# A graph layer's node stage taken apart: its table rows made during the index search, its q and k products beside the edge tiles

## The chip, the cores and the metric

One core of a Trainium2 chip runs the whole program. Its engines work in parallel, each through its own queue of instructions, and meet at semaphores: TensorE (PE in the rows; PEld is its weight load), VectorE (DVE), ScalarE (ACT), GpSimd (POOL) and SyncE (SP, which here only starts DMA transfers). The metric is the device time of one execution in microseconds.

## The reference

One layer over 6250 nodes of 256 channels and 106250 directed edges, sorted by destination. With xn the row-normalised x, it computes x + GNN(xn) + MIX(xn), and then adds a routed expert network of the result.

```python
h = (x @ W.T).reshape(n, H, D)                      # GNN, x is xn
alpha = einsum(h_src, a_src) + einsum(h_dst, a_dst)
enc = relu(edge_attr @ edge_W.T + edge_b)
alpha = alpha + sum(enc * h_dst, axis=-1)           # then leaky relu, softmax over each node's edges
out = segment_sum(h_src * attn[..., None], dst)     # + bias
q, k, v = split(x @ W_qkv + b_qkv)                  # MIX, x is xn
q = q - mean(q); k = k - mean(k); q2 = q*q; k2 = k*k
k2 = l2_normalize(k2 / (sum_c k2 + 1e-7), over nodes)
q2 = l2_normalize(q2 / (sum_c q2 + 1e-7), over channels)
out = (v + q2 @ (k2.T @ v) / sqrt(N)) @ W_out + b_out
```

The experts: a second normalisation, the two best of 8 per node, gelu between two products.

## The kernel before, in words

Nodes are worked on in 49 tiles of 128 (NT; the last has 106). The program is a series of blocks; between two blocks all engines meet at a barrier.

**The search** (lines 233 to 520). For each node the place of its first edge in the sorted list is found in two steps: a coarse count against every 277th destination (L377, DVE), then the row of 277 destinations is gathered for each node (L300, POOL, 49 indirect DMAs) and counted (L437). PE gives each node its successor's value (L326, L327), so that its degree is known (L444). Nodes are then ranked by degree with large one-hot tables on DVE (L449 to L470) and PE (L329 to L336), so that a tile holds nodes of like degree. At the same time DVE and ACT split the edge attributes into three bf16 parts (`records`, L396 to L410, and L346) and SP writes them to DRAM (`recs`). DVE also centres the weights (L386 to L394) and PE makes two small weight products (L314 to L321): `wmo` folds W_v and W_out into one.

**The node stage** (L523 to L732). x is loaded, and for each tile, in an overlapped loop over tiles with buffers for two: DVE normalises (L670 to L676), PE turns the rows (L585) and makes three products (L594): q and k (`wqk`, 512 columns), the table row (`whs`, 272 columns: h and its two attention parts), and v through W_out (`wmo`). ACT and DVE square and scale q and k (L639 to L647, L684 to L708). PE adds the tile into k2.T @ xn and two column sums that stay in PSUM (L603 to L607). SP stores the table rows (L565) and q2 (L567). After the last tile the sums become `kvo` (L621, L721 to L732), which the router needs.

**The edge stage** (L743 to L1003), in the order of ranked tiles. POOL fetches for tile t+1 the edge records (L801) and the destinations' table rows (L803), and gathers one table row per edge slot for 128 nodes at a time (L807, up to 36 slots). Slots go in groups of four; a tile has between 2 and 9 groups (GMAX), 230 in all 49 tiles, and steps of a group above the second stand in an `If` on a number that each engine loads from `info`. PE turns the records (L845), ACT copies them out of PSUM (L902, L904), PE encodes a group's attributes (L854, `encode`), DVE makes the scores (L932, L935, `score`), ACT the exponentials (L917), DVE the weighted rows (L943, `weigh`), and PE sums them (L863, `collect`). Scores of tile t+1 and weights of tile t alternate on DVE. The rows of a tile go to one of two halves of `hbuf`: POOL waits at a tile's start until DVE has weighed the tile before last (`msg_ready`). DVE clears `hbuf` first (L993).

**The router** adds the aggregated rows and q2 @ kvo (L1335) to x; the experts follow.

The order on each engine is the order in which the code is written. The steps touched are those of the search and edge blocks on all five engines.

## Time and profile before

| | us |
|---|---|
| median of 3 runs (lowest, highest) | 3477.73 (3471.06, 3493.76) |
| the profiled execution | 3464.38 |
| its span | 3462.6, granted clock 0.775 in the mean |
| DVE busy | 1726.2 |
| PE busy | 2056.6 |
| POOL busy | 1251.7 |
| ACT busy | 500.4 |

A row of a timeline that ends in brackets tells how long the engine had been idle and what ended it: an engine's instruction, a transfer (DMA), `issue` (nothing that the profile shows) or `remote` (an event without a known sender).

### The profile page before, as it was taken

The numbers are of one execution on the slowest core, as the hardware profiler recorded it, in microseconds if no ns is written. First come the engines' busy times: TensorE is split into PE (matmuls) and PEld (weight loads), VectorE is DVE, ScalarE is ACT, GpSimd is POOL, SyncE is SP. The second block draws the span as 40 slices with busy tenths as digits, with TensorE's granted clock in tenths as the row PEclk, the third lists the DMA queues.
The fourth block names the chain that finished last, engine by engine and source line by source line (L and its number), as shares of the span: only waits on it lengthen the run. The fifth ranks groups of instructions, "written<-read, shape, count | busy, mean of one in ns | idle before, by whom it ended". The sixth has DMA issues, their size and how long they took to land. (4 is left out here: it accounts for less than half of the span.)

```text
span 3462.6 us, 35916 instructions
## 1 busy us (share of the span) xinstructions
PE 2056.6 (59%) x8311; PEld 1568.4 (45%) x8312; DVE 1726.2 (50%) x3708; ACT 500.4 (14%) x1336; POOL 1251.7 (36%) x1251
## 2 busy tenths in 40 slices
PE   0038887355555455444444444445555999999996
PEld 0026555233333333333333322224444888888885
DVE  5756666667655566555555555465453112221221
ACT  0103333000000000000000000002222222222221
POOL 5000000555555555544555544433543221222211
PEclk9569999566666667766666677677566999999998
DMA  4121111333333333322333322224332222322223
GB/s 129 79 80 39 37 37 39 91 87 95 92 88 83 88 93 88 88 78 76 85 87 84 89 74 74 79 59 164 115 112 89 59 60 60 62 37 57 58 39 98
DMA packets 145579, 270.85 MB, mean 78 GB/s; under 512 B 27546, under 2 KB 104068, under 8 KB 144708
## 3 DMA queue, kind: packets, MB, share of 16 engines
q0 software_dynamic: 71312, 179.36, 20.7%
q1 hardware_dynamic: 66292, 77.89, 7.0%
q10 hardware_dynamic: 7872, 12.58, 1.1%
q14 instruction: 82, 0.67, 0.1%
q8 instruction: 21, 0.34, 0.0%
HBM read 208.02 MB, written 68.11 MB: 80 GB/s over the span
## 5 line engine op out<-in xcount | busy, mean ns | idle before, releaser
L807 POOL DMA_INDIRECT hbuf<-table,recb x847 | 805.8, 951 | 736.7 <-issue 689.1
L863 PE MATMUL psum<-msg,ident 128*128 128x256 f32 x1840 | 639.9, 515 | 690.2 <-DVE msg L943 533.0
L863 PEld LDWEIGHTS psum<-msg,ident 128*128 128x128 f32 x1840 | 475.5, 267 | 879.6 <-DVE msg L943 602.3
L932 DVE SCALAR_TENSOR_TENSOR prod<-psum,hd 128x1024 f32<-128x1024 f32 x230 | 281.1, 1222 | 276.8 <-remote 210.5
L943 DVE TENSOR_TENSOR msg<-hbuf,psum 128x1024 f32<-128x1024 f32 x230 | 274.8, 1212 | 248.0 <-remote 235.4
L1378 PE MATMUL psum<-f_xT,fw 128*128 128x256 f32 x1664 | 380.3, 387 | 26.9 <-issue 14.7
L1315 POOL DMA_INDIRECT acc<-yo,id_now x104 | 161.4, 1552 | 633.9 <-DVE yo L1587 606.7
L1388 PE MATMUL psum<-fw,hT 128*128 128x256 f32 x1664 | 367.8, 379 | 0.0
L1378 PEld LDWEIGHTS psum<-f_xT,fw 128*128 128x128 f32 x1664 | 322.3, 194 | 77.8 <-issue 19.1
L1388 PEld LDWEIGHTS psum<-fw,hT 128*128 128x128 f32 x1664 | 312.1, 190 | 40.3
L935 DVE TENSOR_REDUCE al<-prod 128x32 f32<-128x1024 f32 x230 | 280.6, 1220 | 7.9
L1429 ACT ACTIVATE hT<-psum,fb 128x256 f32<-128x256 f32 x416 | 195.0, 473 | 592.2 <-PE psum L1378 531.7
L902 ACT COPY recT<-psum 128x512 bf16<-128x512 bf16 x49 | 28.7, 585 | 1479.0 <-PE psum L845 873.2
L854 PE MATMUL psum<-ew,recT 128*128 128x512 bf16 x460 | 180.1, 506 | 60.2 <-ACT recT L904 21.6
L801 POOL DMA_INDIRECT recb<-recs,stg x49 | 46.6, 951 | 448.8 <-ACT stg L898 399.7
L1574 DVE COPY id_now<-id_next 128x2 int32<-128x2 int32 x52 | 8.8, 169 | 361.7 <-POOLq L1318 359.5
L1584 DVE TENSOR_TENSOR yo<-psum,fb 128x256 f32<-128x256 f32 x104 | 44.1, 424 | 212.7 <-PE psum L1388 212.7
L1303 POOL DMA_INDIRECT xs<-xstage,pstage x98 | 95.9, 978 | 132.5 <-DVEq L1495 104.8
L845 PE MATMUL psum<-ident_bf,recb 128*128 128x128 bf16 x441 | 42.2, 256 | 167.0 <-issue 150.6
L594 PE MATMUL psum<-wqk,xT 128*128 128x512 f32 x196 | 102.2, 646 | 29.6 <-ACT xT L633 29.6
L845 PEld LDWEIGHTS psum<-ident_bf,recb 128*128 128x128 bf16 x441 | 32.0, 115 | 189.8 <-issue 171.8
L854 PEld LDWEIGHTS psum<-ew,recT 128*128 128x128 bf16 x460 | 49.9, 118 | 123.6 <-issue 41.6
(304 smaller groups left out, 2295.8 us busy)
## 6 DMA issues: line engine op xcount, KB each, us to landing
xr<-xs SPq DMA_DIRECT2D x53, 260.0 KB, 2.7
hbuf<-table,recb POOLq DMA_INDIRECT x847
fw<-in_w ACTq DMA_DIRECT2D x12, 1024.0 KB
table<-tab SPq DMA_DIRECT2D x49, 136.0 KB
recs<-rec SPq DMA_DIRECT2D x3, 2216.0 KB, 6.7
q2d<-q2r SPq DMA_DIRECT2D x49, 128.0 KB, 1.7
aggs<-oo SPq DMA_DIRECT2D x49, 128.0 KB
qrow<-q2d SPq DMA_DIRECT2D x49, 128.0 KB
```

The source lines that it names most:

```text
L594: mm = pe.matmul(ps[:, 0:width], xT[:, b, P * o:P * o + P], w[:, o, :], start=(o == 0), stop=(o == 1))
L807: pool.indirect_dma_start(hbuf[:, b, s, :], None, table, bass.IndirectOffsetOnAxis(ap=rec_i[:, b, s, REC // 2 - 1:REC // 2], axis=0)).then ...
L854: mm = pe.matmul(psum[:, 1024 * (k % 2) + 512 * q:1024 * (k % 2) + 512 * q + 512], recT[:, b, k, :], ew[:].rearrange("p s c -> p (s c)")[: ...
L863: mm = pe.matmul(AC[:, 0:C], ident[:], msg[:, k % 2, s, :], start=(k == 0 and s == 0), stop=False, skip_group_check=True)
L932: v.scalar_tensor_tensor(out=prod[:, k % 2, :, :], in0=Z[k % 2], scalar=0.0, in1=bc(hd[:, b, 0:C], 1, GS), op0=ALU.max, op1=ALU.mult).then ...
L935: v.tensor_reduce(al[:, b, GS * HEADS * k:GS * HEADS * (k + 1)], prod[:, k % 2, :, :].rearrange("p s (h d) -> p (s h) d", h=HEADS), AX.X, ...
L943: v.tensor_tensor(msg[:, k % 2, :, :].rearrange("p s (h d) -> p s h d", h=HEADS), hbuf[:, b, s, 0:C].rearrange("p s (h d) -> p s h d", h=H ...
L1303: pool.indirect_dma_start(xs, bass.IndirectOffsetOnAxis(ap=pstage[:, i % 2, k, j:j + 1], axis=0), xstage[:, s, :], None).then_inc(st_x[s], 16)
L1315: pool.indirect_dma_start(acc, bass.IndirectOffsetOnAxis(ap=id_now[:, r:r + 1], axis=0), yo[:, r, :], None, compute_op=ALU.add).then_inc(s ...
L1378: mm = pe.matmul(HB[m % 4][:, 0:FT], fw1[:, e % 2, o, P * m:P * m + P], xT[:, o, :], start=(o == 0), stop=(o == 1))
L1388: mm = pe.matmul(bank[5 + r][:, 0:C], hT[:, m, P * r:P * r + P], fw2[:, e % 2, m, :], start=(m == 0), stop=(m == FM - 1))
L1429: act.activation(hT[:, m, :], HB[m % 4][:, 0:FT], ACT.Gelu, bias=fb1[:, FM * e + m:FM * e + m + 1]).then_inc(gelu_done, 1)
```

## The change

The node stage is gone. Its parts go to two places. In the search block x is loaded early, DVE takes the statistics of seven tiles at a time between the pieces of the coarse search, ACT normalises and makes the copies out of PSUM, and PE runs a loop of 49 tiles, written out, that makes the table row and v; bias and x are added to v by matmuls in PSUM, so that ACT's copy puts the finished row into `xm`. The normalised rows are also stored (`xnd`). ACT takes over the casts of the edge attributes and starts their stores. In the edge block SP loads a tile of normalised rows per edge tile, PE turns it, makes q and k behind the third `encode`, and adds the sums of the tile before at the end of the tile; ACT squares and scales; q2 is stored without its row factor, which the router applies (`qscale`). The records are turned in one PSUM bank (8 blocks, then the ninth) to make room for the accumulators. Only the parts of `hbuf` that must be zero are cleared. The closing steps stand behind the last edge tile.

```diff
-                        for k in range(3):
-                            sp.wait_ge(rec_copied, k + 1)
...
-                            sp.dma_start(recs_v[:, RG * k:RG * k + RG, :], rec[:]).then_inc(st_rec, 16)
-                        sp.wait_ge(st_rec, 48)
...
+                        for c in range(2, NT // NC):
+                            load_x(c)
+
+                        for t in range(NT):
+                            sp.wait_ge(xn_ready, t + 1)
+                            sp.dma_start(xnd[t * P:t * P + P, :], xn[:, t % 4, :]).then_inc(st_xn[t % 4], 16)
+                            sp.wait_ge(tab_ready, t + 1)
+                            sp.dma_start(table[t * P:t * P + P, :], tab[:, t % 2, :]).then_inc(st_tab[t % 2], 16)
...
-                        pe.wait_ge(prep_ready, 1)
+                        pe.wait_ge(ld_w, 16 * 8)
+                        pe.wait_ge(rep_ready, 1)
...
                         mm.then_inc(prep_mm, 1)
+                        pe.wait_ge(prep_ready, 1)
+
+                        for t in range(NT + 1):
+                            if t < NT:
+                                pe.wait_ge(xn_ready, t + 1)
+                                after(pe, xt_ready, t - 1)
+                                for o in range(2):
+                                    mm = pe.transpose(XT[t % 2][:, P * o:P * o + P], xn[:, t % 4, P * o:P * o + P], ident[:])
+                                mm.then_inc(xt_mm, 1)
+                            s = t - 1
+                            if s >= 0:
+                                pe.wait_ge(xt_ready, s + 1)
+                                after(pe, tab_ready, s - 1)
+                                for o in range(2):
+                                    mm = pe.matmul(HP[s % 2], xT[:, s % 2, P * o:P * o + P], whs[:, o, :], start=(o == 0), stop=(o == 1))
+                                mm.then_inc(h_mm, 1)
+                                after(pe, m_added, s - 1)
+                                pe.matmul(MP[s % 2], ones[0:1, :], bmo[0:1, :], start=True, stop=False, skip_group_check=True)
+                                pe.matmul(MP[s % 2], ident[:], xm[:, s, :], start=False, stop=False, skip_group_check=True)
+                                for o in range(2):
+                                    mm = pe.matmul(MP[s % 2], xT[:, s % 2, P * o:P * o + P], wmo[:, o, :], start=False,
+                                                   stop=(o == 1), skip_group_check=True)
+                                mm.then_inc(m_mm, 1)
...
+                        pe.wait_ge(m_added, NT)
...
+                                act.activation(xn[:, t % 4, :], xm[:, t, :], ACT.Identity, bias=off[:, t:t + 1],
+                                               scale=rs[:, t:t + 1]).then_inc(xn_ready, 1)
+                            s = t - 1
+                            if 0 <= s < NT:
+                                act.wait_ge(xt_mm, s + 1)
+                                after(act, m_mm, s - 1)
+                                act.copy(xT[:, s % 2, :], XT[s % 2]).then_inc(xt_ready, 1)
+                            s = t - 2
+                            if 0 <= s < NT:
+                                act.wait_ge(h_mm, s + 1)
+                                after(act, st_tab[s % 2], 16 * (s // 2))
+                                act.copy(tab[:, s % 2, :], HP[s % 2]).then_inc(tab_ready, 1)
+                                act.wait_ge(m_mm, s + 1)
+                                act.copy(xm[:, s, :], MP[s % 2]).then_inc(m_added, 1)
...
+                        for c in range(NT // NC):
+                            ts = slice(NC * c, NC * c + NC)
+                            act.wait_ge(var_ready, c + 1)
+                            act.activation(sd[:, ts], mv[:, ts, 1], ACT.Sqrt, bias=eps[:, 0:1]).then_inc(sd_ready, 1)
+                            pieces[c]()
+                            for t in range(3 * c, 3 * c + 3):
+                                step(t)
...
+                                ch.step(v.bn_stats(st[:, t - NC * c, :], xm[:, t, :]))
+                            for t in range(NC * c, NC * c + NC):
+                                ch.lag(NC - 1)
+                                ch.step(v.bn_aggr(mv[:, t, :], st[:, t - NC * c, :]))
+                            ch.wait()
+                            v.sem_inc(var_ready, 1)
...
+                        ch.run(v.tensor_tensor(bmo[:], bout[:], gbias[:], ALU.add))
+                        v.sem_inc(rep_ready, 1)
+                        blocks(1)
+                        stats(0)
+                        norm(0)
+                        v.wait_ge(prep_copied, 1)
+                        ch.run(v.tensor_tensor(bmo[:], bmo[:], bvo[:], ALU.add))
+                        v.sem_inc(prep_ready, 1)
+                        pieces = {1: (0, 0), 2: (0, 1), 4: (1, 0), 5: (1, 1)}
+                        for c in range(1, NT // NC):
+                            stats(c)
+                            if c + 1 < NT // NC:
+                                blocks(c + 1)
+                            norm(c)
+                            if c in pieces:
+                                rest(*pieces[c])
...
-            with ExitStack() as nd:
...
+                            after(sp, q_ready, t + 1)
+                            sp.dma_start(q2d[bass.ds(t * P, P), :], qsq[:]).then_inc(st_q, 16)
+                            if not is_last(t):
+                                after(sp, g_mm, t)
+                                load(t + 1, 1 - b)
...
+
+                        def project(t):
+                            after(pe, xte_ready, t + 1)
+                            pe.matmul(QK[:], ones[0:1, :], bqk[0:1, :, :].rearrange("p a c -> p (a c)"), start=True, stop=False,
+                                      skip_group_check=True)
+                            for o in range(2):
+                                mm = pe.matmul(QK[:], xTe[:, P * o:P * o + P], wqk[:, o, :, :].rearrange("p a c -> p (a c)"),
+                                               start=False, stop=(o == 1), skip_group_check=True)
+                            mm.then_inc(qk_mm, 1)
...
+                        def sums(t, b, n):
+                            after(pe, k4_ready, t + 1)
+                            for o in range(2):
+                                pe.matmul(GP[:, C * o:C * o + C], xrow[0:n, b, P * o:P * o + P], kn[0:n, :],
+                                          start=False, stop=False, skip_group_check=True)
+                                pe.matmul(CP[:, o:o + 1], kn[0:n, P * o:P * o + P], ones[0:n, 0:1],
+                                          start=False, stop=False, skip_group_check=True)
+                                mm = pe.matmul(CP[:, 2 + o:3 + o], k4[0:n, P * o:P * o + P], ones[0:n, 0:1],
+                                               start=False, stop=False, skip_group_check=True)
+                            mm.then_inc(g_mm, 1)
...
                             n, before = groups_of(pe, t), 0 if is_at(t, 0) else groups_before(pe, t)
+                            after(pe, sq_done, t)
...
                                 turn(t + 1, 1 - b)
-                                after(pe, rec_ready, 2 * t + 4)
+                                after(pe, rec_ready, 2 * t + 3)
                                 for k in range(2):
                                     encode(1 - b, k, upto)
+                                turn_last(t + 1, 1 - b)
+                            transposed(t, b)
...
+                                if k == 2:
+                                    project(t)
                                 with pe.If(n > k):
                                     collect(b, k, before)
-
+                            if not is_at(t, 0):
+                                sums(t - 1, 1 - b, P)
...
+                        sums(NT - 1, (NT - 1) % 2, LAST)
...
+                        def squares(t):
+                            after(act, qk_mm, t + 1)
+                            act.activation(ksq[:], QK[:, C:2 * C], ACT.Square, accum_out=ksum[:]).then_inc(ksq_ready, 1)
+                            after(act, st_q, t * 16)
+                            act.activation(qsq[:], QK[:, 0:C], ACT.Square,
+                                           accum_out=qsum[:, bass.ds(t, 1), 0]).then_inc(q_ready, 1)
+                            after(act, q_ready, t + 1)
+                            act.activation(QK[:, C:2 * C], qsq[:], ACT.Square,
+                                           accum_out=qsum[:, bass.ds(t, 1), 1]).then_inc(sq_done, 1)
...
+                            after(act, g_mm, t - 1)
                             act.activation(pr[:, 0:CAP * HEADS], al[:, b, 0:CAP * HEADS], ACT.Exp).then_inc(exp_ready, 1)
+                            after(act, xt_mm, t + 1)
+                            act.copy(xTe[:], QK[:, 0:C]).then_inc(xte_ready, 1)
+                            if not is_at(t, 0):
+                                scaled(t - 1)
+                            squares(t)
...
                             if not is_at(t, 0):
+                                factor(t - 1)
...
-                        v.memset(hbuf[:], 0.0).then_inc(hbuf_clear, 1)
+                        v.memset(prod[:, 0, :, :], 0.0).then_inc(zero_ready, 1)
+                        v.memset(hbuf[:, :, 0:GS - 1, :], 0.0).then_inc(hbuf_clear, 1)
+                        v.memset(hbuf[:, :, GS - 1:CAP, C:C + HEADS], 0.0).then_inc(hbuf_clear, 1)
...
-                            v.tensor_tensor(row, row, MX[f % 2][:, 0:C], ALU.add).then_inc(x2_ready, 1)
+                            v.scalar_tensor_tensor(out=row, in0=MX[f % 2][:, 0:C], scalar=qscale[:, f:f + 1], in1=row,
+                                                   op0=ALU.mult, op1=ALU.add).then_inc(x2_ready, 1)
```

On PE, in the search block before: the small weight products (L321) are followed by the successor matmuls (L326, L327).

```order
L314 MATMUL psum<-wout,wvT 128x256 x4
L317 MATMUL psum<-wout,bvrep 128x256 x2
L321 MATMUL psum<-asd,wh 128x16 x4
L326 MATMUL psum<-first,shift 128x49
L327 MATMUL psum<-first,wrap 128x49
L329 MATMUL psum<-small,tri 128x64
```

PE at the end of the same block's table loop, now (L371 is the table product, L374 bias, L375 x, L377 v):

```order
L377 MATMUL psum<-wmo,xT 128x256 x2
L371 MATMUL psum<-whs,xT 128x272 x2
L374 MATMUL psum<-bmo,ones 128x256
L375 MATMUL psum<-xm,ident 128x256
L377 MATMUL psum<-wmo,xT 128x256 x2
L382 MATMUL psum<-first,shift 128x49
L383 MATMUL psum<-first,wrap 128x49
```

The successor matmuls (L382, L383) now stand behind the loop of 49 tiles.

PE in one tile of the edge loop before, down to the third group:

```order
L845 MATMUL psum<-ident_bf,recb 128x128 x9
L77 REGISTER_ALU
L854 MATMUL psum<-ew,recT 128x512 x4
L77 REGISTER_ALU
L863 MATMUL psum<-msg,ident 128x256 x4
L77 REGISTER_ALU
L863 MATMUL psum<-msg,ident 128x256 x4
L880 COMPARE_AND_BRANCH
L77 REGISTER_ALU
L854 MATMUL psum<-ew,recT 128x512 x2
L880 UNCONDITIONAL_BRANCH
L882 COMPARE_AND_BRANCH
```

The same tile now (L833 turns x, L838 and L841 are bias and the q and k product):

```order
L833 MATMUL psum<-ident,xrow 128x128 x2
L78 REGISTER_ALU
L826 MATMUL psum<-msg,ident 128x256 x4
L78 REGISTER_ALU
L826 MATMUL psum<-msg,ident 128x256 x4
L872 COMPARE_AND_BRANCH
L78 REGISTER_ALU
L817 MATMUL psum<-ew,recT 128x512 x2
L872 UNCONDITIONAL_BRANCH
L838 MATMUL psum<-bqk,ones 128x512
L841 MATMUL psum<-wqk,xTe 128x512 x2
L876 COMPARE_AND_BRANCH
```

The new product has moved in between the third group's encode (L817) and its collect.

## Rows read from the trace of the kernel before

**Rows 1.** Stages: stretch, its us, busy us and instructions per engine, clock, DMA share, GB/s

```profile
0.00:142.90 142.90, 8.57 (x26) 6.22 (x27) 86.82 (x277) 17.58 (x8) 47.10 (x54) 0.78 0.36 126
142.90:214.40 71.50, 15.53 (x102) 15.15 (x102) 60.75 (x69) 0.00 (x0) 0.49 (x1) 0.60 0.00 0
214.40:239.40 25.00, 2.29 (x4) 1.17 (x4) 0.78 (x3) 1.28 (x1) 0.00 (x0) 0.50 0.81 256
239.40:598.60 359.20, 298.11 (x1282) 212.60 (x1282) 234.65 (x890) 122.20 (x491) 0.00 (x0) 0.96 0.11 37
598.60:621.80 23.20, 3.46 (x15) 1.44 (x15) 18.61 (x4) 1.51 (x4) 1.91 (x2) 0.50 0.07 19
621.80:2350.30 1728.50, 829.13 (x2728) 555.87 (x2726) 1018.80 (x1179) 83.40 (x194) 896.89 (x943) 0.69 0.31 84
```

**Rows 2.** Timeline, search stage: start, us, engine, line, operation, output<-input, idle before

```profile
50.21 0.17 DVE L380 TENSOR_SCALAR blk<-blk 128x7 f32<-128x7 f32 x1 [7.64 <-issue]
...
71.28 3.78 PE L314 MATMUL psum<-wout,wvT 128*128 128x256 f32 x8 [62.85 <-issue]
...
73.89 1.26 POOL L300 DMA_INDIRECT rows_b<-in_dst,blki  x1 [0.30 <-issue]
...
142.93 0.21 DVE L444 TENSOR_TENSOR deg<-psum,first 128x49 f32<-128x49 f32 x1 [1.24 <-PE psum L327]
...
216.69 5.49 SPq L557 DMA_DIRECT2D xm<-in_x  x3
```

**Rows 3.** Timeline, PE in one tile of the node stage

```profile
405.67 1.96 PE L594 MATMUL psum<-wqk,xT 128*128 128x512 f32 x4 [0.61 <-ACT xT L633]
...
407.46 1.08 PE L594 MATMUL psum<-whs,xT 128*128 128x272 f32 x4
...
408.38 1.03 PE L594 MATMUL psum<-wmo,xT 128*128 128x256 f32 x4
...
409.25 0.59 PE L603 MATMUL psum<-k2n,xn 128*128 128x256 f32 x2
...
410.69 0.36 PE L607 MATMUL psum<-ones,k 128*128 128x1 f32 x2
```

**Rows 4.** Groups of the node stage: count, busy us, mean ns, idle before and its releaser

```profile
L585 PE MATMUL psum<-ident,xn 128*128 128x128 f32 x98 | 21.6, 303 | 47.1 <-DVE xn L676 47.1
...
L633 ACT COPY xT<-psum 128x256 f32<-128x256 f32 x49 | 18.2, 372 | 126.7 <-PE psum L585 126.7
```

**Rows 5.** Timeline, PE in the node stage's first tile

```profile
242.31 3.78 PE L594 MATMUL psum<-wqk,xT 128*128 128x512 f32 x4 [0.46 <-ACT xT L633]
```

**Rows 6.** Timeline, end of the node stage and start of the edge stage, DVE

```profile
591.33 0.16 DVE L721 COPY cols<-psum 128x4 f32<-128x4 f32 x1 [1.05 <-PE psum L607]
...
602.75 16.38 DVE L993 MEMSET hbuf<- 128x19584 f32 x1 [4.62 <-issue]
...
620.09 1.22 DVE L932 SCALAR_TENSOR_TENSOR prod<-psum,hd 128x1024 f32<-128x1024 f32 x1 [0.34 <-issue]
```

**Rows 7.** Groups of the edge stage, DVE's waits

```profile
L932 DVE SCALAR_TENSOR_TENSOR prod<-psum,hd 128x1024 f32<-128x1024 f32 x229 | 279.9, 1222 | 276.5 <-remote 210.5 <-PE psum L854 41.5 <-issue 19.1
...
L943 DVE TENSOR_TENSOR msg<-hbuf,psum 128x1024 f32<-128x1024 f32 x230 | 274.8, 1212 | 248.0 <-remote 235.4 <-PE psum L863 12.5
```

**Rows 8.** Timeline of the edge stage at four places

```profile
716.56 1.22 DVE L943 TENSOR_TENSOR msg<-hbuf,psum 128x1024 f32<-128x1024 f32 x1 [2.81 <-PE psum L863]
...
1200.72 0.95 POOL L807 DMA_INDIRECT hbuf<-table,recb  x1 [0.30 <-issue]
...
1204.76 1.22 DVE L943 TENSOR_TENSOR msg<-hbuf,psum 128x1024 f32<-128x1024 f32 x1 [7.36 <-remote]
...
1210.96 0.94 POOL L807 DMA_INDIRECT hbuf<-table,recb  x1 [9.30 <-issue]
...
2300.34 1.23 DVE L932 SCALAR_TENSOR_TENSOR prod<-psum,hd 128x1024 f32<-128x1024 f32 x1 [25.36 <-remote]
```

**Rows 9.** The page's list of transfers

```profile
q2d<-q2r SPq DMA_DIRECT2D x49, 128.0 KB, 1.7
```

507 lines of the change are left out of this document (236 added, 271 removed).

## The prediction

> **What bounds the kernel now.** I read the stages first, then each stage's own limit. The split by stages [rows 1] has six rows: the search for node boundaries up to 142.9 us, its ranking part up to 214.4, a load of x, the node stage (359.2 us), the clearing of hbuf, and the edge stage (1728.5 us); routing and the experts follow and hardly change. The reader should see two things. In the ranking part PE and ACT work for 15.5 and 0.0 of 71.5 us, and in the first part for 8.6 and 17.6 of 142.9. The node stage is the reverse: PE is busy 298 of 359 us at a granted clock of 0.96, and POOL and the DMA engines do next to nothing. In the edge stage no engine is full: DVE 1019 of 1728 us, PE 829, POOL 897, ACT 83.
>
> The timeline of one node tile [rows 3] shows what a tile costs on PE when its parts follow one another: the q and k product starts at 405.67, the table product at 407.46, the v product at 408.38, the sums at 409.25, and the last of the sums ends at 410.69 + 0.36 = 411.05. So q and k take 1.79 us, the table 0.92, v 0.87 and the sums 1.80. With the two turns (21.6 / 49 = 0.44, [rows 4]) that is 5.8 of the 359.2 / 49 = 7.3 us of a tile.
>
> The edge stage's limit is a loop through three engines [rows 8]. POOL issues its last gather of a burst at 1200.72 and then waits for DVE's products; DVE has stood still for 7.36 us and goes on at 1204.76, 3.1 us after that gather was issued; POOL starts the next burst at 1210.96. At 2300.34 DVE has waited 25.36 us for the end of a burst. These waits, whose releaser the profile doesn't know (it writes remote), sum to 210.5 + 235.4 = 446 us ahead of DVE's two large instructions [rows 7], 9 us for each of 49 tiles. The early tiles are without them; there DVE waits for PE (2.81 us at 716.56, [rows 8]).
>
> **The change, part by part.**
>
> *Removed: the node stage.* The next stage starts at 598.6 instead of some 3 us behind the search (a barrier: the search ends at 214.3 here and x is asked for at 216.69, [rows 2]). What remains of the node work must fit in the search stage and in the edge stage.
>
> *Added to the search: the table loop on PE.* PE does per tile two turns (0.44), the table product (0.92), and the sum of bias, x and v. The last is twice the matmuls of the v product alone (0.87), so 1.74. Sum: 3.10 us if nothing waits; by the node stage's busy times, which include each drain, 3.6. I take 3.3, so 49 x 3.3 = 162 us. ACT carries four copies of 256 to 272 columns per tile at 0.37 [rows 4], about 1.6 us with their gaps, under PE's 3.3, plus some 25 us of record casts. DVE adds 49 pairs of statistics, about 30 us, to a part in which it had 56 of 142.9 us free: hidden. The loop starts when weights, the first seven tiles of x and their statistics are there: PE's small products take about 6 us before, DVE's first statistics about 5 after two blocks of boundary search. I put it at 38 us. It ends at 200; with 5 us for the casts that stand in ACT's queue between the copies, at 205.
>
> *What waits for it.* The matmul that gives each node its successor stands behind the whole loop in PE's queue (the first piece of order above). Before, DVE had its answer at 142.93 [rows 2]; now at 205 + 1.3 = 206. DVE itself would be ready near 130. Behind it stand the ranking steps, unchanged: 71.5 us to the end of the block. So the edge stage starts at 206 + 71.5 + 3 = 280.5 instead of 598.6: **-318 us**.
>
> *Clearing.* The fill of all of hbuf takes 16.38 us [rows 6] and DVE's first score waits for it (620.09). The new fills are 2 x 3 x 272 and 2 x 33 x 8 columns, 2160 of 19584, so 1.8 us, and prod's 0.9: **-14 us**.
>
> *Added to the edge tile.* On PE: two turns of x (0.44), a bias matmul (0.45), q and k (1.79), sums (1.80): 4.5 us at the high clock. At the low clock q and k took 3.78 us against a busy time of 1.95 in the steady tile [rows 5], a factor of 1.94, so 8.7 us. The product goes behind the third encode; there PE stands still while DVE waits for the burst, 7 us in the tile shown, so it is covered. The sums come at the tile's end, before the next tile's records are turned: 1.8 to 3.5 us, of which about 1 us is slack ahead of DVE's score. DVE gets two one-column steps, 0.4 us with their gap. So DVE reaches its long wait about 2.5 us later, and since that wait ends with the burst, the tile isn't longer. Where no such wait stands (the first half dozen tiles, and the last) I count 4 us each, 28, and 2 for odd ones: **+30 us**. If the cover were gone, all 4.9 us would be on the path in 49 tiles: 240. SP gets a store and a load of 128 KB per tile; the load waits for the sums of the tile before and is wanted after the next tile's second encode, some 5 us later, against 1.7 us for such a transfer to land [rows 9]. POOL's queue gets nothing.
>
> *Moved to the end.* The closing steps (from 591.33 to 598.1, [rows 6]) now stand behind the last edge tile, and ACT loads a table for them: 6.8 and a little over 1 for that, **+8 us**. The router's scaling rides in an instruction that was there: 0.
>
> The sum: 3464.4 - 318 - 14 + 30 + 8 = 3170 us in the profiled execution's measure. That execution was 13.3 us under the median of the three runs shown, 3477.7, so I predict **3184 us**.
>
> **Operations that this trace doesn't show.** A matmul with one row of weights (the biases): between nothing and a full one of the same columns; I take the full one, which its streamed columns suggest (0.45 and 0.22 us each; low end -32 us over both loops). ACT's record copies are the same 1152 columns in two pieces, cut elsewhere: taken as equal; they lie ahead of the covered wait either way. A start of the table loop before 25 us isn't possible (weights and statistics), after 75 neither (next paragraph).
>
> **A rule against the edge part.** In the search stage DVE stood still for 7.64 us before L380 in straight code, waiting for nothing but its own instruction, while POOL issued row gathers; PE began its products at 71.28, near the last gather at 73.89 [rows 2]. The same may befall the new unrolled loops. The Trainium skill (Runtime: NRT & Kernel Launch, Instruction fetch mechanics) says that straight code is fetched ahead and its fetch mostly hidden, and that a taken branch whose target isn't resident stalls for a DMA. By that rule the unrolled table loop would be free of such stalls and the sum stays as it is, while the edge loop, now longer on PE and ACT, could get new ones; the row at L380 speaks against the first half.
>
> **Rivals.**
> - *The table loop is held by the row gathers.* PE gets going only as the gathers end, at 75 instead of 38, as its first product did in this trace. +37: 3221. It speaks for it that PE waited until 71.28; against it, that PE then waited for DVE. 13%.
> - *The table loop runs at the low clock or in a handshake with ACT.* 3.3 x 1.94 = 6.4 us per tile, +152: 3336. The node stage held 0.96 with PE busy 83%, and the loop is denser. 6%.
> - *The edge additions aren't covered, at the high clock.* 49 x 4.9 = 240 in place of 30: 3394. 6%.
> - *Slower than before.* The added matmuls run at the low clock (the edge stage's granted clock is 0.69) and the wait of DVE isn't tied to the burst but to PE or to DVE's own code, so that everything added lies on the path: 8.7 + 0.4 + 1.5 for exp, which is now behind the ninth record block on ACT. 49 x 10.6 = 520 in place of 30: 3674. It decides from 6.6 us of exposed work per tile on: (3477.7 - 3184 + 30) / 49. 4%.
> - *Full exposure between these two*, within 1% of before: 3%.
> - *A warmer PE shortens the edge stage.* DVE's waits for PE there (41.5 + 12.5 = 54 us, [rows 7]) go as PE is less idle: 3184 - 30 - 54 = 3100. 8%.
>
> That the change doesn't do what it says isn't likely: the order of instructions shows the node loop gone. The forecast keeps 60%.
>
> **Range and chances.** The forecast's own range is 3130 to 3245: -32 for cheap biases, -20 for an earlier start, +37 and some tiles more for the other side. To hold 8 in 10 the range takes in the warmer edge stage's half and reaches toward the slow table loop: 3105 to 3310. Differences under 1% can't be told from no change here. Faster by more than 1%: all cases but two, 0.93; within 1%: 0.03; slower: 0.04.
>
> **What will show it.** The first successor matmul's answer near 206 us; PE busy over 90% from 40 to 205 us at a clock above 0.9; first staging copy of the edge stage near 280; first score 6 to 9 us behind it; an edge stage of 1755 us or so from the first gather on, with DVE's unexplained waits shorter by about 2.5 us each. I'm wrong if PE has gaps in the table loop, if DVE's waits in the edge stage keep their length while its other work grows, or if PE's new project step shows before DVE's fourth score.

## The result: 0.943 of the kernel before

The changed kernel takes 3277.96 us (median of 4 runs, 3275.74 to 3294.0) against 3476.05 us before on the same chip: ratio 0.9431, 95% interval 0.9407 to 0.9455. The forecast was 3184 us with a range of 3105 to 3310, so the gain was 198 us and not 292. The time lies outside the forecast's own range of 3130 to 3245 and inside the wide one. The profiled execution spans 3274.2 us against 3462.6; these two are compared below.

The split by stages of the changed kernel answers to [rows 1]. Columns: stretch, its length, busy time of PE, its weight loads, DVE, ACT and POOL, granted clock, DMA share, GB/s.

```profile
0.00:26.00 26.00, 7.75 (x22) 5.54 (x23) 16.75 (x72) 5.46 (x10) 9.94 (x14) 0.96 0.86 280
26.00:154.00 128.00, 94.49 (x325) 62.26 (x325) 75.28 (x305) 62.88 (x113) 39.21 (x40) 0.79 0.49 166
154.00:241.90 87.90, 87.90 (x366) 61.46 (x366) 0.00 (x0) 38.71 (x104) 0.00 (x0) 0.96 0.29 105
241.90:317.70 75.80, 15.38 (x104) 14.88 (x103) 60.76 (x69) 0.24 (x2) 0.48 (x1) 0.62 0.00 0
326.10:2158.10 1832.00, 1036.51 (x3718) 691.64 (x3716) 1035.82 (x1294) 211.86 (x639) 893.92 (x942) 0.72 0.32 86
2158.10:3274.20 1116.10, 896.72 (x4156) 773.44 (x4156) 308.47 (x1287) 274.56 (x639) 305.16 (x251) 0.88 0.32 78
```

The table loop has two halves. From 154 us on PE is busy without a gap; in the 128 us before it is busy 94.5 at a clock of 0.79. Then DVE ranks with little work on the other engines, as before. Against the kernel before:

| stretch | before | after | difference |
|---|---|---|---|
| up to the first staging copy of the edge stage | 598.6 | 317.7 | -280.9 |
| from there to DVE's first score | 21.5 | 8.45 | -13.0 |
| first score to the last tile's output | 1726.3 | 1816.3 | +90.0 |
| from there to the router's first gather | 4.6 | 15.6 | +11.0 |
| router and experts | 1111.6 | 1116.1 | +4.5 |

**The search stage.** Eight rows of the changed kernel's timeline (start, length, engine, line, operation; in brackets how long the engine had been idle and what ended it):

```profile
145.65 1.89 ACT L431 CAST rec<-att 128x831 bf16<-128x831 f32 x1 [3.96 <-DVE att L494]
147.57 5.28 ACT L436 COPY rec<-rec 128x2493 bf16<-128x2493 bf16 x2
...
151.78 0.21 DVE L582 SCALAR_TENSOR_TENSOR first<-blk,fine 128x49 f32<-128x49 f32 x1
...
153.98 0.69 PE L364 MATMUL psum<-ident,xn 128*128 128x128 f32 x2 [9.44 <-ACT xn L407]
...
238.72 0.37 ACT L420 COPY xm<-psum 128x256 f32<-128x256 f32 x1 [1.73 <-PE psum L377]
241.76 0.37 ACT L420 COPY xm<-psum 128x256 f32<-128x256 f32 x1 [1.73 <-PE psum L377]
242.14 0.21 DVE L586 TENSOR_TENSOR deg<-psum,first 128x49 f32<-128x49 f32 x1 [90.15 <-PE psum L383]
...
317.68 0.29 ACT L907 COPY stg<-fetch 128x2 int32<-128x2 int32 x2 [75.56 <-PEq L169]
```

ACT casts the last piece of a third of the records, copies it twice (5.28 us) and issues its store. PE has no normalised tile in this time and stands 9.44 us. From 160.53 on ACT's copies of the finished row (`xm`) come 3.25 us apart, 26 of them, and the loop ends at 242. DVE had its first positions at 151.78 and waited 90.15 us for the successor product, which stands behind the loop on PE. The answer at 242.14 and the 75.5 us of ranking behind it give the start.

**The edge stage.** The costliest groups that answer to [rows 7], and ACT's and POOL's (busy and mean ns of one; idle time before them by releaser). The name `DMA srci<-in_src` is that of a semaphore number used earlier in the program: the profile knows no sender, as where it writes `remote`.

```profile
L769 POOL DMA_INDIRECT hbuf<-table,recb x847 | 805.1, 951 | 527.3 <-issue 511.8 <-DVE msg L985 15.5
L974 DVE SCALAR_TENSOR_TENSOR prod<-psum,hd 128x1024 f32<-128x1024 f32 x230 | 281.4, 1223 | 563.4 <-DMA srci<-in_src 373.2 <-PE psum L817 150.3 <-issue 33.9
L985 DVE TENSOR_TENSOR msg<-hbuf,psum 128x1024 f32<-128x1024 f32 x230 | 278.4, 1211 | 39.4 <-remote 24.1 <-PE psum L826 9.2 <-ACT psum L942 5.6
L911 ACT COPY recT<-psum 128x1024 bf16<-128x1024 bf16 x49 | 49.6, 1012 | 784.1 <-DMA bndi<-in_dst 632.3 <-PE psum L806 105.0 <-issue 46.8
L763 POOL DMA_INDIRECT recb<-recs,stg x49 | 46.3, 944 | 348.5 <-issue 246.5 <-DVEq L1004 82.0 <-ACT stg L907 20.0
```

DVE's idle time ahead of its two large instructions rose from 524.5 us to 602.8, which is 78 of the 90 us. Its unexplained part fell (446 to 397), but the waits for PE's encode rose from 41.5 to 150.3. The tile at 837.9 us shows why:

```profile
837.86 0.62 PE L806 MATMUL psum<-ident_bf,recb 128*128 128x128 bf16 x8 [1.10 <-issue]
837.88 0.46 DVE L1002 TENSOR_TENSOR al<-al,mask 128x288 f32<-128x288 f32 x1 [2.20 <-issue]
...
841.97 0.94 POOL L769 DMA_INDIRECT hbuf<-table,recb  x1 [0.30 <-issue]
...
844.56 1.01 ACT L911 COPY recT<-psum 128x1024 bf16<-128x1024 bf16 x1 [12.03 <-DMA bndi<-in_dst]
845.62 1.89 PE L817 MATMUL psum<-ew,recT 128*128 128x512 bf16 x4 [7.15 <-ACT recT L911]
846.69 1.23 DVE L974 SCALAR_TENSOR_TENSOR prod<-psum,hd 128x1024 f32<-128x1024 f32 x1 [4.13 <-PE psum L817]
...
847.82 0.20 ACT L907 COPY stg<-fetch 128x2 int32 x1
...
849.79 0.94 POOL L763 DMA_INDIRECT recb<-recs,stg  x1 [6.88 <-issue]
...
852.28 0.95 POOL L769 DMA_INDIRECT hbuf<-table,recb  x1 [0.30 <-issue]
...
860.55 0.59 PE L817 MATMUL psum<-ew,recT 128*128 128x512 bf16 x2
...
871.05 0.94 POOL L769 DMA_INDIRECT hbuf<-table,recb  x1 [0.30 <-issue]
...
875.21 1.22 DVE L974 SCALAR_TENSOR_TENSOR prod<-psum,hd 128x1024 f32<-128x1024 f32 x1 [15.54 <-DMA srci<-in_src]
```

PE turns the records at the tile's start, but ACT's first record copy comes 6.7 us later, 1.6 us behind the end of POOL's burst. The staging copy stands behind the second record copy, which needs PE's ninth transpose, which stands behind four encode matmuls: 3.3 us behind the first copy (before the change 1.1, in the tile at 939.2 us of its trace, below). So POOL fetches the next records 11.9 us into the tile, its late burst starts so late that the next tile's first eight gathers follow without a gap (16 gathers, 852.28 to 871.99), and DVE's last score waits to their end plus 3.2 us. PE's encode for that score (L817, the row at 860.55) had been done at 861.1 us. The next tile is short: in this pair 42.4 and 25.5 us stand where two of 31.5 stood.

```profile
941.08 0.58 ACT L902 COPY recT<-psum 128x512 bf16<-128x512 bf16 x1 [25.63 <-PE psum L845]
941.62 0.69 ACT L904 COPY recT<-psum 128x640 bf16<-128x640 bf16 x1
942.20 0.20 ACT L898 COPY stg<-fetch 128x2 int32 x1
```

The pairs aren't all of the 90 us. Tile by tile against the kernel before, 9 us lie in the first 5 tiles, 44 in the next 16, where the long and short tiles alternate, 28 in the 10 behind them, and 5 in the 17 after those.

### The profile page after: what moved, and what is told of

The parts are those of the page before. It is cut to its first block and busy times, and to the rows that moved or that the text cites. A ratio compares the mean times of both kernels' runs of the same rounds, so it can differ in the third digit from the quotient of the medians.

```text
span 3274.2 us, 35308 instructions
## 1 busy us (share of the span) xinstructions
PE 2143.4 (65%) x8703; PEld 1611.7 (49%) x8704; DVE 1500.5 (46%) x3029; ACT 595.3 (18%) x1505; POOL 1252.5 (38%) x1251
## 3 DMA queue, kind: packets, MB, share of 16 engines
q0 software_dynamic: 71312, 179.36, 22.0%
## 5 line engine op out<-in xcount | busy, mean ns | idle before, releaser
L826 PE MATMUL psum<-msg,ident 128*128 128x256 f32 x1840 | 590.5, 484 | 454.0 <-DVE msg L985 453.0
L826 PEld LDWEIGHTS psum<-msg,ident 128*128 128x128 f32 x1840 | 450.9, 250 | 600.6 <-DVE msg L985 489.1
L817 PE MATMUL psum<-ew,recT 128*128 128x512 bf16 x460 | 172.1, 487 | 190.5 <-ACT recT L911 179.8
L985 DVE TENSOR_TENSOR msg<-hbuf,psum 128x1024 f32<-128x1024 f32 x230 | 278.4, 1211 | 39.4 <-remote 24.1
L911 ACT COPY recT<-psum 128x1024 bf16<-128x1024 bf16 x49 | 49.6, 1012 | 784.1 <-DMA bndi<-in_dst 632.3
L817 PEld LDWEIGHTS psum<-ew,recT 128*128 128x128 bf16 x460 | 47.4, 113 | 247.7 <-ACT recT L911 188.6
L923 ACT ACTIVATE ksq<-psum 128x256 f32<-128x256 f32 x49 | 18.8, 383 | 606.4 <-remote 289.9
L841 PE MATMUL psum<-wqk,xTe 128*128 128x512 f32 x196 | 97.2, 618 | 0.0
```

The lines of the kernel that those rows point to most:

```text
L817: mm = pe.matmul(psum[:, 1024 * (k % 2) + 512 * q:1024 * (k % 2) + 512 * q + 512], recT[:, b, k, :], ew[:].rearrange("p s c -> p (s c)")[: ...
L826: mm = pe.matmul(AC[:, 0:C], ident[:], msg[:, k % 2, s, :], start=(k == 0 and s == 0), stop=False, skip_group_check=True)
L841: mm = pe.matmul(QK[:], xTe[:, P * o:P * o + P], wqk[:, o, :, :].rearrange("p a c -> p (a c)"), start=False, stop=(o == 1), skip_group_che ...
L985: v.tensor_tensor(msg[:, k % 2, :, :].rearrange("p s (h d) -> p s h d", h=HEADS), hbuf[:, b, s, 0:C].rearrange("p s (h d) -> p s h d", h=H ...
```

## The experiments

"Stage" is the time from the first staging copy to the router's first gather: 1752.4 us before (14 of it the clearing of hbuf), 1840.4 in the changed kernel. The runs fell on other chips than the prediction's. The kernel before took 3530.6, 3523.7 and 3527.8 us on the three chips of runs 1 to 4, 5 to 8 and 9 to 11, so these three are compared with each other, though the expectations of the third speak of one chip. "Ratio" is to the kernel before on the run's own chip, with its 95% interval.

| run | start of stage | stage | ratio |
|---|---|---|---|
| 5 the changed kernel again | 323.5 | 1861.6 | 0.9392 (0.936 to 0.9425) |
| 1 no node work | 319.7 | 1699.6 | 0.9007 (0.8973 to 0.9041) |
| 2 staging copy first | 318.5 | 1786.7 | 0.9171 (0.9135 to 0.9207) |
| 3 ranking inside the loop | 265.0 | 1865.6 | 0.9222 (0.9192 to 0.9253) |
| 4 before, with ACT filler | 608.8 | 1805.7 | 1.0035 (1.0019 to 1.0051) |
| 6 plain loads | 321.1 | 1424.9 | 0.8155 (0.813 to 0.8181) |
| 7 no node work, two banks | 321.5 | 1779.2 | 0.9231 (0.9203 to 0.926) |
| 8 three edits | 276.3 | 1783.6 | 0.9039 (0.9007 to 0.9071) |
| 9 pause on POOL | 322.5 | 1848.8 | 0.938 (0.935 to 0.9409) |
| 10 three edits, spread | 241.1 | 1784.6 | 0.8965 (0.8932 to 0.8997) |
| 11 no node work, staging first | 318.5 | 1766.0 | 0.9215 (0.9183 to 0.9246) |
| 12 twelve gathers first | 234.4 | 1385.0 | 0.9074 (0.9054 to 0.9094) |

In runs 1, 6, 7 and 11 the router gets other rows, and in runs 1, 7 and 11 the part from its first gather on is 18 to 25 us longer than in run 5; of these four only the stage is read.

**Run 1, no node work.** `transposed`, `project`, `sums`, `scaled`, `squares` and `factor` are gone from the tiles, with SP's load of the normalised rows, and q2d's store writes a constant.

```diff
-                            after(pe, sq_done, t)
...
-                            transposed(t, b)
...
-                                if k == 2:
-                                    project(t)
...
-                                sums(t - 1, 1 - b, P)
```

> The changed kernel without the node work in its edge tiles: the xn row's load and transposes, the q and k products, the three squares, the scaled copies, the factor and the sums are left out (so the global branch gets no sums, and the router sees other rows); what stays is the record turn through one bank, the last transpose behind two encodes, and DVE's new order. Read from the first staging copy to the router's first gather, which is 1840.4 us in the changed kernel and 1752.4 in the one before (1738 without the clearing of hbuf). Theory A, the node work itself delays the tiles: 1730 to 1760. Theory B, the one-bank turn with its last copy behind two encodes delays them: it stays at 1815 to 1840. A mixture lies between, and its place gives the shares.

Measured 1699.6, below theory A's range; theory B, that the one-bank turn alone costs the time, is out. But ACT's first record copy is still late in many tiles (8.3 us into the one at 862.4), and in the tile of the same number as the one at 837.9 POOL's bursts run together as there: 18 issues without a gap, from 814.36 to 836.57. Four rows:

```profile
814.36 0.94 POOL L759 DMA_INDIRECT recb<-recs,stg  x1 [6.84 <-issue]
...
829.11 1.23 DVE L956 SCALAR_TENSOR_TENSOR prod<-psum,hd 128x1024 f32<-128x1024 f32 x1 [4.92 <-DMA srci<-in_src]
829.37 0.95 POOL L765 DMA_INDIRECT hbuf<-table,recb  x1 [0.30 <-issue]
...
835.62 0.95 POOL L765 DMA_INDIRECT hbuf<-table,recb  x1 [0.30 <-issue]
```

DVE's wait ends here after 4.92 us, in the middle of the gathers, and the pair takes 34.7 and 25.4 us. So bursts that run together don't by themselves make the tiles long.

**Run 2, staging copy first.** `turned_last` is the second half of `turned`, the wait for PE's ninth transpose and the copy behind it.

```diff
                                 after(act, ld_hd[b], 8 * (t - b) + 16)
                                 stage(t + 2, b)
+                            if not is_last(t):
+                                turned_last(t + 1, 1 - b)
                             after(act, al_ready, t + 1)
```

> The changed kernel with ACT's staging copy issued between the two record copies, ahead of the one that waits for PE's last transpose. In the tile at 837.9 us the staging copy was 3.3 us behind the first record copy, where it was 1.1 behind it before the change. If the late staging copy is what starts POOL's second burst late, and so ends DVE's wait late: 2 us less in each of 47 tiles, 90 us of the 1840 at most, 3190 us in all. If ACT's first record copy is what is late (it came 6.7 us behind the tile's start, where it was 1.9 before), the gain is small: under 25 us, 3255 to 3278.

The stage is 75 us shorter than run 5's, 1.6 us a tile. The tile of the same number, at 817.2 us:

```profile
825.17 1.01 ACT L911 COPY recT<-psum 128x1024 bf16<-128x1024 bf16 x1 [13.24 <-DMA bndi<-in_dst]
826.08 0.20 ACT L907 COPY stg<-fetch 128x2 int32 x1
...
828.05 0.94 POOL L763 DMA_INDIRECT recb<-recs,stg  x1 [4.62 <-issue]
...
839.30 0.95 POOL L769 DMA_INDIRECT hbuf<-table,recb  x1 [0.30 <-issue]
841.54 1.23 DVE L979 SCALAR_TENSOR_TENSOR prod<-psum,hd 128x1024 f32<-128x1024 f32 x1 [4.84 <-DMA srci<-in_src]
...
846.11 0.94 POOL L769 DMA_INDIRECT hbuf<-table,recb  x1 [5.86 <-DVE msg L990]
```

The record copy comes no earlier (8.0 us in), but the staging copy is 0.9 behind it, the late burst stands alone, and DVE's wait ends behind 8 gathers and not 16. This tile and the next take 33.0 and 31.1 us. Part of the gain has another place: 21 of the 75 us lie in the last 17 tiles, where the changed kernel was only 5 us longer than the one before.

**Run 3, ranking inside the loop.**

```diff
                         for t in range(NT + 1):
+                            if t == 24:
+                                next_nodes()
+                            if t == 28:
+                                counts()
+                            if 39 <= t < 39 + NT // NC:
+                                metas_of(t - 39)
...
-                        pe.matmul(bank[4][:, 0:NT], shift[:], first[:, 0:NT], start=True, stop=False)
```

> The changed kernel with the ranking's matmuls put inside PE's table loop: the successor product ahead of tile 24, the counts ahead of tile 28, the seven pieces of the places in tiles 39 to 45, their results in banks 4 and 5. In the changed kernel DVE had its first positions at 151.8 us and waited 90.2 us for the successor product, which stands behind the whole loop. If that order is what made the edge stage start at 317.7: DVE's ranking now runs beside the loop, the loop ends near 258 (16 us more on PE), the edge stage starts at 258 to 268, and the time is 3220 to 3228. If something else held the start (the loop's own pace, POOL), the start moves by less than 15 us.

The start is 265.0, as expected: 58.5 us ahead of run 5's, and 53.5 ahead of run 2's on the same chip. The stage itself stayed (1865.6).

**Run 4, the kernel before with a longer ACT program.**

```diff
+                            after(act, filled, 8 * t)
+                            for j in range(8):
+                                act.copy(spare[:, 8 * j:8 * j + 8], ident[:, 8 * j:8 * j + 8]).then_inc(filled, 1)
```

> The kernel before the change, with eight tiny ACT copies (128x8, from a constant to a spare buffer) behind each tile's Exp, where ACT has over 20 us to spare. They add about 1.6 us of ACT work a tile beside DVE's work, and no one waits for them. If a tile's length hangs only on who waits for whom, the time is that of the kernel before, 3460 to 3480. If a longer ACT program in the tile makes ACT itself stall while POOL gathers (as its record copy does in the changed kernel, 6.7 us into the tile at 837.9), the edge stage is longer by 0.5 to 2 us a tile: 3490 to 3570.

The time is 12 us longer, 0.25 a tile: under the 0.5 to 2 us of the second expectation, but not nothing. ACT's record copies still come 0.1 to 1.9 us into the tile. So eight more copies on ACT don't make them late. The run also gives an estimate of the kernel before's stage on these chips: 1805.7 - 12 - 14 of clearing = 1780.

**Run 5, the changed kernel again**, the reference of the table.

> The changed kernel as it is, for a reference on the chip of the other runs (chips differ: the kernel before took 3476 us on one and 3531 on another). Both theories: 0.943 of the kernel before.

**Run 6, plain loads.**

```diff
                                     for s in range(GS * k, GS * k + GS):
-                                        gather(b, s)
+                                        pool.dma_start(hbuf[:, b, s, :], table[0:P, :]).then_inc(ld_h[b], 16)
```

> The changed kernel with the row gathers of each tile's third and later groups replaced by plain transfers of the same size and the same 128 descriptors (always the table's first 128 rows, so the messages are of other rows), issued by POOL. In the changed kernel DVE's last score of a tile waits 9 to 15 us until 3.2 us behind the end of POOL's burst of gathers, and no instruction packet is moved from 500 to 2100 us. If the burst of indirect gathers on POOL is what holds the other engines: the long waits shrink by most of the 8 to 13 gathers' 1.25 us each, the 4-group tiles go from 32 us to 20 to 26, and the edge stage is 300 us or more shorter. If it is the traffic of the rows that holds them, or the other engines' own chain that makes the tile, the edge stage stays within 60 us of 1840.

```profile
L793 POOL DMA_DIRECT2D hbuf<-table x528 | 284.8, 586 | 2.0 <-issue 1.8
L974 DVE SCALAR_TENSOR_TENSOR prod<-psum,hd 128x1024 f32<-128x1024 f32 x230 | 281.4, 1223 | 190.4 <-PE psum L817 176.5 <-issue 6.4 <-DMA srci<-in_src 1.3
L911 ACT COPY recT<-psum 128x1024 bf16<-128x1024 bf16 x49 | 49.6, 1012 | 533.9 <-DMA bndi<-in_dst 335.1 <-PE psum L806 138.2 <-issue 60.6
```

The stage is 437 us shorter with as many bytes (179.36 MB on POOL's queue in both); the 4-group tiles take 25 to 29 us, a little more than expected. DVE's waits without a sender ahead of its scores fell from 389.9 us (run 5) to 1.3. What stays is ACT's late record copy, which follows the first eight gathers, still indirect. So the long waits go with the bursts of indirect gathers, and not with the number of bytes. Two things changed besides: the rows read are always the same 128, and POOL issues one in 0.59 us and not 1.25, some 349 us less in all. Which of the three frees the engines (the index, the choice of rows or the shorter issue) no run parts. Nor are instructions fetched for them: of the queues, the changed kernel's traffic from 900 to 1500 us has these two and no instruction queue (it moves 107 such packets in the whole program).

```profile
DMA packets 22667, 52.77 MB, mean 88 GB/s; under 512 B 5810, under 2 KB 12082, under 8 KB 22667
...
q0 software_dynamic: 15611, 46.35, 28.8%
q1 hardware_dynamic: 7056, 6.43, 3.3%
```

**Run 7, no node work, two banks**: run 1 with `turn` and `turned` as in the kernel before (nine transposes in banks 4 and 7, the staging copy behind both copies).

> The run without the node work (its first staging copy to the router's first gather took 1699.6 us) with the record turn as before the change: nine transposes into two banks, the encodes behind both copies, the staging copy right behind the copies. Same parts left out as there. If ACT's late record copies (up to 8 us into a tile) come from the one-bank turn: the copies come 1 to 2 us into the tile again, and the stage is 30 to 100 us shorter, 1600 to 1670. If they come from elsewhere (DVE's new order, SP's second store in the tile): 1690 to 1710, and the copies still come late.

The copies come 0.1 to 1.8 us into the tile again, as the first theory has it, and yet the stage is 80 us longer than run 1's, which no theory had. Nor is the one-bank turn alone what makes the copies late: in run 11, which has it, most come 0.4 to 2.2 us into the tile. 1779.2 is what the kernel before has here by the estimate (1780): DVE's new order, with the row sum between the first two `weigh`, shows no gain.

**Run 8, three edits together**: run 2, run 3 and ACT's order in the search block.

```diff
-                            pieces[c]()
-                            for t in range(3 * c, 3 * c + 3):
+                            for t in range(2 * c, 2 * c + 2):
                                 step(t)
...
+                        pieces = {14: (0, 0), 16: (0, 1), 18: (0, 2), 22: (1, 0), 24: (1, 1), 26: (1, 2), 30: (2, 0), 32: (2, 1), 34: (2, 2)}
```

> The changed kernel with three edits. (1) The staging copy between the record copies, as tried alone: 0.974 of the changed kernel by the ratios to the kernel before. (2) The ranking's matmuls inside PE's table loop (successor ahead of tile 31, counts ahead of 34, places in tiles 43 to 49). (3) ACT's order in the search block: the seven square roots with two tiles each between them, then the casts of the records one every second tile, where in the changed kernel PE stood 4 to 10 us beside every cast in its first 128 us and did 22 tiles in them. If ACT's order is what paced the loop: the loop runs at 3.26 us a tile from 26 us on and with the ranking's 16 us ends near 205 to 215, the edge stage starts at 208 to 225, the time is 3085 to 3110 on the chip of the prediction, 0.885 to 0.897 of the kernel before. If DVE or the row gathers pace it: the start is at 235 to 260, 0.90 to 0.91.

The start at 276.3 is outside both ranges, later than run 3's. PE still stood 5.4 to 6.7 us ahead of 118.3, 154.2 and 191.4, each time behind a block of 8 us on ACT (1.91 for a cast, 5.25 for two copies, two issues), and DVE stood 19.9 us for a cast. An earlier gap of 8.4 us, ahead of 82.7, has no such block before it; it lies beside the row gathers. The ratio, 0.9039, lies in the range of the second expectation.

**Run 9, a pause on POOL**: `pause` fills a spare buffer of 128x2048, which takes 1.82 us.

```diff
                         def tile(t, b):
+                            pause(t)
                             n = groups_of(pool, t)
```

> The changed kernel with a memset on POOL (128x2048, to a spare buffer) at the start of each of its tiles, between the late gathers of one tile and the first eight of the next, which in the changed kernel run together (16 gathers without a gap, 852 to 872 us) in every second tile. If what costs the time is that the bursts run together (the other engines' waits end 3.2 us behind a burst's end), the pause splits them, the pairs of tiles become alike, and the edge stage is shorter than the 1862 us of the changed kernel on this chip: 1780 to 1840. If POOL's issuing itself bounds the stage, each pause adds its own length, 1 to 3 us in 49 tiles: 1900 to 2010.

The stage is 13 us shorter and not 90 longer, outside both ranges; the ratio, 0.938 against 0.9392, can't be told from run 5's. The 1.82 us of each of 49 pauses, 89 us in all, cost nothing: POOL's own issue time isn't the bound, it has slack between bursts. Nor is the running together of the bursts what costs the time: the pause parts them, and where they had run together (4-group tiles) the pairs are 1 to 5 us shorter and still unlike (38.7 and 27.9 us). In the first of these two DVE's wait ends at 871.42 us, in the middle of the eight gathers behind the pause.

**Run 10, the casts spread.**

```diff
+                        pieces = {14: (cast, 0, 0), 16: (cast, 0, 1), 17: (cast, 0, 2), 18: (tail, 0, 1), 19: (tail, 0, 2),
+                                  22: (cast, 1, 0), 23: (cast, 1, 1), 24: (cast, 1, 2), 25: (tail, 1, 1), 26: (tail, 1, 2),
+                                  29: (cast, 2, 0), 33: (cast, 2, 1), 36: (cast, 2, 2), 37: (tail, 2, 1), 38: (tail, 2, 2)}
```

> The run with all three edits (edge stage started at 276.3 us there), with ACT's long pieces parted: each cast and each of the two tail copies of the records stands alone between two tiles, DVE's subtractions stand later in its scans, and the ranking's matmuls stand ahead of tiles 27, 30 and 41 to 44. In that run PE stood 6 to 9 us four times beside blocks of 8 us on ACT (a cast, two tail copies, two issues), and DVE stood 30 us for casts. If these blocks pace the loop: no PE gap over 4 us behind 85 us, the loop ends at 210 to 225, the edge stage starts at 215 to 235, 40 to 60 us earlier, 0.887 to 0.893 of the kernel before. If the first 85 us (row gathers, DVE's order) hold it, the start moves by under 20 us.

```profile
124.27 1.02 DVE L503 TENSOR_TENSOR att<-att,rec 128x831 f32<-128x831 f32 x1 [7.90 <-ACT rec L442]
...
132.18 1.89 ACT L442 CAST rec<-att 128x831 bf16<-128x831 f32 x1 [2.81 <-DVE att L503]
...
134.47 0.44 PE L391 MATMUL psum<-ident,xn 128*128 128x128 f32 x2 [2.25 <-ACT xn L418]
...
241.05 0.29 ACT L917 COPY stg<-fetch 128x2 int32<-128x2 int32 x2 [4.42 <-PEq L169]
```

No PE gap over 2.4 us behind 85 us, and the start is 35 us earlier, a little short of the 40 to 60: the loop ended at 236.2, because the first 10 tiles, up to 85 us and beside the row gathers, had taken 5.9 us each. The run also moves DVE's subtractions and the ranking's matmuls, so the 35 us aren't those of ACT's pieces alone. It is the fastest version on these chips: 0.8965 / 0.9392 = 0.955 of the changed kernel, and faster than both kernels.

**Run 11, no node work, staging first.**

> The run without the node work, with the staging copy between the record copies. From the first staging copy to the router's first gather the changed kernel took 1861.6 us on this chip, 1786.7 with the staging copy moved, 1699.6 without the node work, so each edit alone gives 75 and 162. If the two act on different waits they add up: 1620 to 1635. If the late staging copy costs time only because the node work makes the tile long, or the other way round, the second edit gives little: 1680 to 1700. Same parts left out as in the other run without node work.

1766.0: the edit that takes 75 us off with node work adds 66 without it. Both expectations fell. The rows of runs 1 and 11 for POOL's record fetch, in this order:

```profile
L759 POOL DMA_INDIRECT recb<-recs,stg x49 | 46.3, 945 | 262.4 <-issue 195.1 <-DVEq L986 47.3 <-ACT stg L896 20.0
```

```profile
L759 POOL DMA_INDIRECT recb<-recs,stg x49 | 46.9, 957 | 67.3 <-issue 32.4 <-ACT stg L896 20.0 <-DVEq L991 7.6
```

In run 1 POOL waits 195 us more before its fetches and its bursts fall elsewhere in the tile. Why that is better there and worse with node work is open. The four stages together (run 5, 2, 1 and 11):

| stage | staging copy late | staging copy early |
|---|---|---|
| with node work | 1861.6 | 1786.7 |
| without | 1699.6 | 1766.0 |

**Run 12, twelve gathers first**, on run 10.

```diff
+                            with pool.If(n > 2):
+                                for s in range(2 * GS, 3 * GS):
+                                    gather(b, s)
...
-                            for k in range(2, GMAX):
+                            for k in range(3, GMAX):
```

> The fastest version so far (0.8965 of the kernel before; edge stage from first staging copy to router's gather 1784.6 us), with POOL gathering a tile's third group with its first two, ahead of the next tile's record fetch, and only the later groups behind it: the late burst, at whose end plus 3.2 us DVE's last wait ends, is 4 or 8 gathers instead of 8 or 12, and the next tile's burst is 12 instead of 8. If the end of the late burst is what DVE's last wait hangs on, it ends up to 5 us earlier in the tile, less what the later record fetch gives back: 1680 to 1750 us. If the whole of POOL's issues per tile counts, wherever it stands: 1770 to 1800. If the longer burst reaches into the next tile's start and holds ACT's record copy there (5 us later): 1850 to 2000.

This run fell on a chip on which the kernel before took 2940.8 us, and can't be read against the others. But it shows something larger:

```profile
L992 DVE SCALAR_TENSOR_TENSOR prod<-psum,hd 128x1024 f32<-128x1024 f32 x230 | 281.5, 1224 | 148.6 <-PE psum L830 125.3 <-issue 17.0 <-DMA srci<-in_src 0.3
L1003 DVE TENSOR_TENSOR msg<-hbuf,psum 128x1024 f32<-128x1024 f32 x230 | 278.5, 1211 | 8.3 <-PE psum L839 7.8 <-ACT psum L959 0.5
L924 ACT COPY recT<-psum 128x1024 bf16<-128x1024 bf16 x49 | 49.6, 1012 | 416.5 <-PE psum L819 416.5
```

Every instruction has the length that it has elsewhere (1224, 1211, 1012 ns), but the waits without a sender are gone, on DVE and on ACT, with the same 847 indirect gathers. Since the kernel before, unchanged, is 583 to 590 us faster there too, it is the chip and not the edit that takes away most of them; that is argued from the times, as the kernel before has no trace on that chip.

## Why the prediction was right in sign, and its gain half too large

- **The range.** It holds the time in part by luck: 3310 was set for a slow table loop, and most of what was missed lies in the edge stage.
- **The table loop's start and pace.** The start is 26.2 us, 12 earlier than the 38 forecast; the pace where nothing disturbs it is 3.25 us a tile (3.3), right. So was the full price of the biases: at the high clock the one-row matmul took 0.69 us for its two passes, the 128-row one 0.70.
- **"ACT carries four copies ... under PE's 3.3, plus some 25 us of record casts", with 5 us of them on PE's path: the first step that failed.** The loop ended at 242, not 205, though it began 12 us early. Up to 154 us it had done 22 tiles, 5.8 us each. ACT is one tile ahead of PE, so a block of 8 us on ACT is a gap of 5 to 9 us on PE (9.04, 7.34 and 9.44 in the changed kernel), and the tile behind it runs at the low clock (the copies of `xm` at 154.36 and 160.53 are 6.2 us apart, then 3.3). Run 10, which parts the pieces, starts the stage 35 us before run 8. Another part of the lost time lies beside the row gathers, where the first copies of `xm` come 4.9, 7.2 and 9.0 us apart: the first rival, which I gave 13%, holds for part of it.
- **What waits for it.** Successor answer to first staging copy 75.5 us (74.5 forecast); -318 became -281 for the loop's end alone. Run 3 shows the wait itself as a term of its own: the stage starts 54 to 58 us earlier when the ranking's matmuls move into the loop, where they take 16 us.
- **Clearing and the closing steps.** -13.0 (-14) and +11.0 (+8).
- **The edge tiles, +30, measured +90: the second step that failed**, and the larger. The sentence at fault is the one on ACT's record copies: "taken as equal; they lie ahead of the covered wait either way". They aren't equal: the ninth transpose went behind the encodes, and the staging copy with it. With the staging copy moved back alone (run 2) the stage is 1786.7 us, 7 over the 1780 estimated for the kernel before. So in this kernel its late place costs 75 us. What the node work costs, for which the +30 was worked out, has no single value: 21 us with the staging copy early (run 11 against run 2), 162 with it late (run 1 against run 5). The edges of this account are open: that the time is lost where a late burst meets the next one fits the tile at 837.9, but in run 1 the bursts meet as well and the tiles are short, and run 9 parts them and gains 13 us at most. That POOL waits for ACT's staging copy stood in the code (POOL's `gate(pool, staged, t + 2, passed)` ahead of `fetch_tile`), and I costed "POOL's queue gets nothing" without asking who starts POOL: its waits before the record fetch grew from 49.0 to 328.5 us in all, the first one aside.
- **The signs I had named.** DVE's unexplained waits shrank by 49 us, 1.0 and not 2.5 a tile. PE had gaps in the table loop, a sign of failure that held. The project step (L838, L841 in PE's order) did show before the fourth score at 875.21, at 855.96 us of the tile above, another sign; it wasn't the cause, since the fourth encode behind it was done at 861.1, 14 us before that score. PE over 90% busy from 40 us on: wrong up to 154.
- **A warmer PE** (0.72 against 0.69) brought no gain that shows: DVE's waits for PE's encodes, which that rival had going away, grew from 41.5 to 150.3 us.
- **The rule against the edge part.** In the edge loop DVE, ACT and PE stand still for up to 15.54, 12.24 and 8.53 us around the tile at 837.9, and from 500 to 2100 us the changed kernel moves no instruction packet. The Trainium skill (Runtime: NRT & Kernel Launch, Instruction fetch mechanics) has a taken branch outside the resident pages stall for a DMA. The trace doesn't agree with that as the cause here; besides, longer ACT code gave 12 us (run 4), and the stalls are gone on one chip. What makes them is open. Shown is that they come beside POOL's bursts of indirect gathers, go away with plain transfers of the same size, and depend on the chip. In the changed kernel all 35 such waits of over 4 us ahead of DVE's scores and products end 1.6 to 3.9 us behind a burst's last gather; in the kernel before 16 of 49, and in run 1 12 of 35, end while POOL still issues.

## What to carry to other kernels

When an instruction moves, follow every engine that waits for it in turn, and look at what stands behind it, such as the small copy that lets POOL start its fetches: here a 0.2 us copy, 2.2 us later in its tile, cost 75 us. Work hidden in another engine's slack should be cut into pieces shorter than the slack that the ring of buffers between them holds, and a product that another engine waits for belongs where its operands are ready, not behind the loop. An edit's gain in a stage of coupled waits must be measured with its neighbours in place: the same edit was worth -75 us and +66.

## What was not expected

- Three chips gave the kernel before 3524 to 3531 us, the prediction's chip 3476, and one chip 2941 us. The kernel before has a trace on the prediction's chip only; traces of changed versions show equal instruction lengths on all of them, and on the last chip no waits without a known sender beside the gathers.
- An indirect gather of 128 rows costs POOL 1.25 us (951 ns and 0.30), a plain transfer of the same 128 descriptors 0.59.
- A memset of 1.82 us in each of POOL's 49 tiles changed the time by less than can be told, though in the changed kernel DVE's long waits end behind POOL's bursts.
